# Graph attention over 16 batches: half-width masked tiles and a split store for the last batch, and a new hand-written front

## The chip, the cores and the metric

The kernel runs on one core of a Trainium2 chip. The metric is the device time of one execution in microseconds. TensorE (PE) does products and transposes into eight PSUM banks; VectorE (DVE), ScalarE (ACT) and GpSimd (POOL) do the element-wise work and reductions; SyncE (SP) and ScalarE issue DMAs. Each engine works through its own list in order and meets the others at semaphores.

## The reference

`x` is 16 batches of 512 nodes with 128 features, `adj` a 512 x 512 adjacency. Cut to what is computed:

```
def gat(inp, mask, W, a):
    h = inp @ W
    e = leaky_relu((h @ a_first)[:, :, None] + (h @ a_second)[:, None, :], 0.2)
    if mask is not None: e = where(mask > 0, e, -9e15)
    return elu(softmax(e, axis=2) @ h)

h   = relu(layernorm(x))
out = relu(h @ mlp1_w + mlp1_b)                       # 256 wide
out = elu(gat(out, None, W_fc, a_fc)) + out           # first attention, 256 wide
out = relu(out @ mlp2_w + mlp2_b)                     # 128 wide
out = relu(elu(gat(out, adj, W_hand, a_hand)) + out)  # second attention, masked
x   = x + out
x   = x + gat(relu(layernorm(x)), adj, W, a)          # third attention, masked
```

## The kernel before

Everything is fp32. A batch is four tiles of 128 nodes (`C` = 4). Each batch goes through the same steps, and a step is named `step.batch`: `stats1`, `root1`, `norm1` (or `normt`, on x loaded by features) for the first normalisation; `mlp1_0`, `mlp1_1` for the two 128-wide halves of the first dense layer, kept in `o1_t`; `h1_0` to `h1_3` for the products with `W_fc` of the four node tiles, evicted to `ext`; `max1`, `args1`, `row1` for the scores; `prob1_t` for the unnormalised attention of source tile t to all 512 targets; `att1_c` for the products of target tile c over the four source tiles; `elu1`, `z`, `mlp2`. The second attention is `h2`, `max2`, `args2`, `row2`, `prob2`, `att2`, `elu2`, `x1` (with `turn_o2`), then `norm2`, `root2`, `turn2`; the third is `h3`, `max3`, `args3`, `row3`, `prob3`, `att3`, `elu3`, and `result` writes `y_out`, which SyncE's step `result` stores.

A probability tile holds, for 128 sources in the partitions, all 512 targets in the columns. In the masked layers of batches 13 to 15 (`SCALED`, `HALVED`) ScalarE scales the row of the targets by the sources' factor (`scale_row`, L833), and VectorE takes the maximum with a second factor and the minimum with the mask (`prob_scaled`, L1177). For these batches the row stays in a PSUM bank, filled by four transposes (L1432). TensorE's `attend_masked` (L1493) makes two groups of products, q = 0 for target tiles 0 and 1, q = 1 for 2 and 3. It waits for each of the four probability tiles in turn at the first target tile, so its second target tile needs all four. The tails of the attention (`att3_q`, `elu3_q`, `result_q`) go in halves of 256 columns for batches 13 to 15.

What each engine does when is written out by hand: `ORDER` has one list per engine with every step of every batch, and `sequence` walks through it. A product takes the next of eight banks in the order of TensorE's list and waits until the reader of the step eight places earlier is done (`free`). `STIRRED` puts extra transposes of the identity in front of some steps (L1327), `WARM` seven at the start (L1322). Batch 0 is normalised by the steps `means` and `roots` (transposes of its moments, L1372), batches 1 and 2 by `norm1` and `turn1` (L1363), all others from moments that go through memory.

`edgeless` (L977 to L981) reduces the adjacency over its columns on VectorE; `empties` (L1352) turns its result, and `masks_0` to `masks_3` (L989) make the mask. `scores1` and `scores23` (L1335, L1343) fill the score columns of the weights.

A guard watches the range of the exponents. Its step `flag` (L1258, VectorE) writes `guard_flag`. At the end of its list every engine waits for it, loads it and branches past a general form of the network (L1542, L1543), then drains (L1558). SyncE first waits for all stores (L1541). The steps of VectorE's list end with `elu3_1.15 result_1.15 flag`.

## Time and profile before

| | us |
|---|---|
| median of 3 runs | 432.27 |
| lowest, highest | 432.2, 433.75 |
| profiled execution | 432.44 |
| its span | 430.6 |
| TensorE busy | 411.8 |
| VectorE busy | 358.1 |
| ScalarE busy | 314.4 |

The span runs from the first to the last instruction of the profiled execution; 1.8 us of its time lie outside. Busy time of TensorE is modelled with the end of each product, so products that follow each other overlap by some 0.16 us in the rows: how long a step holds the engine is read from the start of one to the start of the next. An fp32 product is two records, a transpose one.

### The profile page before, as it was taken

How to read it: one execution, taken by the hardware profiler on the slowest of the kernel's cores; microseconds unless marked ns; L12 is line 12 of the kernel's file. 1: busy time of each engine (PE TensorE's matmuls, PEld its weight loads, DVE VectorE, ACT ScalarE, POOL GpSimd, SP SyncE). 2: the span in 40 equal slices, each digit the busy share in tenths (PEclk: the TensorE clock that was granted, in tenths of full speed). 3: DMA queues.
4: the chain of work that ended last, by engine and by line, in shares of the span. 5: the costliest groups of instructions: out<-in, count | busy, mean ns of one | idle time of the engine just before them, and what ended most of it. 6: DMA issues, size and time to landing. Idle time of an engine off the chain costs nothing.

```text
span 430.6 us, 8695 instructions
## 1 busy us (share of the span) xinstructions
PE 411.8 (96%) x2545; PEld 353.0 (82%) x2545; DVE 358.1 (83%) x1222; ACT 314.4 (73%) x760; POOL 25.0 (6%) x53
## 2 busy tenths in 40 slices
PE   6899999999999999999999999999999999989782
PEld 4688788887888989797998788989889799869772
DVE  6788589968888898889898787987798989889973
ACT  2545867778876978686777878479678887799873
POOL 0000000000001000000100010100100110010000
PEclk9999999999999999999999999999999999999998
DMA  7745145142332123232321422223120223101101
GB/s 216 247 150 172 30 115 143 48 112 73 100 122 75 51 99 98 52 100 74 121 76 51 123 57 94 66 63 95 51 74 2 73 77 99 47 4 32 43 2 54
DMA packets 39445, 36.41 MB, mean 85 GB/s; under 512 B 4064, under 2 KB 30304, under 8 KB 39392
## 3 DMA queue, kind: packets, MB, share of 16 engines
q1 hardware_dynamic: 37392, 33.17, 25.8%
q10 hardware_dynamic: 2000, 2.63, 1.9%
q8 instruction: 22, 0.36, 0.3%
q14 instruction: 31, 0.25, 0.2%
HBM read 31.46 MB, written 4.32 MB: 83 GB/s over the span
## 4 chain that ended last, share of the span: by engine, by line
issue 66%; PE 20%; DVE 6%; POOL 5%; ACT 2%; POOLq 0%; DVEq 0%; ACTq 0%
PE bank L1403 6%; POOL fmax L713 5%; PE bank L1392 4%; PE bank L1493 3%; PE bank L1382 2%; DVE prob L1177 2%; PE bank L1421 1%; DVE u L1231 1%; PE bank L1443 1%; PE bank L1432 1%; DVE stats L1010 1%; PE bank L1411 1%; PE bank L1322 0%; ACT e L885 0%; PE bank L1372 0%
## 5 line engine op out<-in xcount | busy, mean ns | idle before, releaser
L1493 PEld LDWEIGHTS bank<-ext,prob 128*128 128x128 f32 x1024 | 119.6, 192 | 5.5 <-issue 3.1
L1493 PE MATMUL bank<-ext,prob 128*128 128x129 f32 x1024 | 122.6, 276 | 0.6 <-DVE prob L1177 0.3
L1403 PE MATMUL bank<-ext,prob 128*128 128x257 f32 x512 | 118.4, 380 | 0.0
L1403 PEld LDWEIGHTS bank<-ext,prob 128*128 128x128 f32 x512 | 95.0, 190 | 16.7 <-issue 4.2
L1177 DVE SCALAR_TENSOR_TENSOR prob<-prob,square,mask_t 128x512 f32<-128x512 f32 x102 | 73.5, 741 | 5.1 <-ACT prob L833 5.0
L1392 PE MATMUL bank<-wfc_sb,o_t 128*128 128x259 f32 x256 | 63.3, 382 | 0.0
L833 ACT ACTIVATE prob<-row,square 128x512 f32<-128x512 f32 x78 | 54.5, 721 | 0.7 <-DMA row<-row_scratch 0.6
L1392 PEld LDWEIGHTS bank<-wfc_sb,o_t 128*128 128x128 f32 x256 | 46.4, 191 | 9.2 <-issue 3.5
L1231 DVE SCALAR_TENSOR_TENSOR u<-e,y 128x512 f32<-128x512 f32 (+1 forms) x70 | 44.6, 639 | 9.5 <-issue 4.7
L877 ACT ACTIVATE y<-bank,recip 128x128 f32<-128x128 f32 x128 | 39.1, 366 | 16.5 <-DVE recip L1223 16.4
L885 ACT ACTIVATE e<-y,minus_one 128x512 f32<-128x512 f32 (+1 forms) x70 | 47.8, 686 | 1.1
L713 POOL PARTITION_ALL_REDUCE fmax<-fmax_col x48 | 24.3, 506 | 390.3 <-DVE fmax_col L1112 390.2
L866 ACT ACTIVATE y<-bank,recip 128x256 f32<-128x256 f32 x64 | 29.6, 465 | 11.7 <-DVE recip L1216 11.6
L889 ACT ACTIVATE e<-e,minus_one 128x512 f32<-128x512 f32 (+1 forms) x51 | 35.6, 697 | 2.4
L1382 PE MATMUL bank<-normed_t,w_sb 128*128 128x512 f32 x64 | 32.5, 594 | 0.0
L1158 DVE TENSOR_SCALAR prob<-row,square 128x512 f32<-128x512 f32 x64 | 32.3, 535 | 0.0
L1421 PE MATMUL bank<-z_t,w_sb 128*128 128x512 f32 x64 | 30.3, 596 | 0.3 <-DVE z_t L1238 0.3
L771 ACT ACTIVATE o_t<-bank,vec_sb 128x512 f32<-128x512 f32 x32 | 21.8, 688 | 10.9 <-issue 4.2
L779 ACT ACTIVATE ext<-bank 128x259 f32<-128x259 f32 x64 | 23.0, 384 | 6.3 <-issue 2.5
L817 ACT ACTIVATE square<-args 128x12 f32<-128x12 f32 x48 | 9.9, 207 | 22.8 <-DVE args L1133 12.1
L1238 DVE SCALAR_TENSOR_TENSOR z_t<-bank,o_t 128x512 f32<-128x512 f32 x32 | 21.5, 683 | 3.4 <-PE bank L1411 3.2
L807 ACT ACTIVATE ext<-bank,rstd 128x131 f32<-128x131 f32 x64 | 19.6, 370 | 3.7 <-PE bank L1443 2.4
(96 smaller groups left out, 496.6 us busy)
## 6 DMA issues: line engine op xcount, KB each, us to landing
row<-row_scratch SPq DMA_DIRECT2D x36, 256.0 KB, 3.3
moments_row<-moments_scratch SPq DMA_DIRECT2D x13, 512.0 KB, 3.9
x_in<-in_x SPq DMA_DIRECT2D x16, 256.0 KB, 4.7
x_res<-in_x SPq DMA_DIRECT2D x16, 256.0 KB, 4.2
out<-y_out SPq DMA_DIRECT2D x16, 256.0 KB, 3.7
normed<-in_x_t SPq DMA_DIRECT2D x14, 256.0 KB, 4.3
row_scratch<-square_t SPq DMA_DIRECT2D x144, 0.5 KB
adj_sb<-in_adj ACTq DMA_DIRECT2D x1, 1024.0 KB, 6.6
```

The lines of the kernel that those rows point to most:

```text
L713: nc.gpsimd.partition_all_reduce(L.fmax[:, b.slot], L.fmax_col[:, b.slot], P, bass.bass_isa.ReduceOp.max).then_inc(s.fmax.sem, 1)
L833: nc.scalar.activation(L.prob_of(b)[:, t], row_of(b, L), ACT.Copy, scale=L.buv[:, b.slot, 2, t:t + 1]).then_inc((s.scaled_first if t == 0 ...
L877: nc.scalar.activation(L.y[:, c], filled[:, e * (D + 3):e * (D + 3) + D], ACT.Copy, bias=1.0, scale=L.recip[:, b.slot, c:c + 1]).then_inc( ...
L885: nc.scalar.activation(L.e[:, r], L.y[:, r], ACT.Exp, bias=minus_one[:]).then_inc(s.exp.sem, 2 // parts)
L889: nc.scalar.activation(L.e[:, r], L.e[:, r], ACT.Exp, bias=minus_one[:]).then_inc(s.exp2.sem, 2 // parts)
L1177: nc.vector.scalar_tensor_tensor(out=p, in0=p, scalar=L.buv[:, b.slot, 1, t:t + 1], in1=mask_t[:, t], op0=ALU.max, op1=ALU.min).then_inc(s ...
L1231: nc.vector.scalar_tensor_tensor(out=L.u[:, r], in0=L.e[:, r], scalar=1.0, in1=L.y[:, r], op0=ALU.min, op1=ALU.max).then_inc(s.u.sem, 2 // ...
L1382: nc.tensor.matmul(filled[:], w1_sb[:, f * P:(f + 1) * P], normed_t[0][:, b.slot], start=True, stop=True).then_inc(o1_filled.sem, 1)
L1392: last = nc.tensor.matmul(filled[:, 0:H + 3], o1_t[:, b.of(O1_DEPTH), k, c * P:(c + 1) * P], wfc_sb[:, k], start=(k == 0), stop=(k == HT - 1))
L1403: last = nc.tensor.matmul(filled[:, 0:H + 1], gat1.targets(b, t, c), gat1.features_and_one(b, t), start=(t == 0), stop=(t == C - 1))
L1421: last = nc.tensor.matmul(filled[:], w2_sb[:, k], z_t[:, b.slot, k], start=(k == 0), stop=(k == HT - 1))
L1493: last = nc.tensor.matmul(filled[:, e * (D + 3):e * (D + 3) + D + 1], L.targets(b, t, c), L.features_and_one(b, t), start=(t == 0), stop=( ...
```

## The change

1. **Half tiles.** `CUT` names batch 15 for the third attention. There each of the four steps `prob3_t.15` makes two pieces of 256 columns: t = 0 the source tiles 0 and 1 for the first 256 targets, t = 1 the tiles 2 and 3 for the same targets, t = 2 and t = 3 the same for the other 256. That is 8 instructions of 256 columns on ScalarE and on VectorE each, where there were 4 of 512. `att3_0.15` waits for the first two steps only, `att3_1.15` for the last two.
2. **Store in halves.** The store of batch 15 is two DMAs, the first as soon as `result_0.15` is done, with a semaphore of its own.
3. **Front by hand.** On TensorE `h1_0.0` and `h1_1.0` stand ahead of `turn1.1`, `h1_2.0` and `h1_3.0` behind it and ahead of `mlp1_0.1`. Stirring before `roots.0` is two transposes, not three. `scores23` is 11 places later, `empties` behind `att1_0.0`. ScalarE evicts `mlp1_0.0` and `mlp1_1.0` before `root1.1`.
4. **Order elsewhere.** The five lists hold the same steps as before, but are listed anew. On TensorE a step moves by 1.4 places in the mean, on ScalarE and VectorE by 2.4. In VectorE's list `flag` stands ahead of `result_0.15`.

```diff
+CUT = {1: (), 2: (15,)}
-STIRRED = {("roots", 0): 3, ("mlp1_0", 0): 3, ("row3", 14): 10, ("turn2_half", 15): 6, ("h3_0", 15): 4}
+STIRRED = {("roots", 0): 2, ("mlp1_0", 0): 3, ("row3", 14): 10, ("turn2_half", 15): 6, ("h3_0", 15): 4}
...
     "scalar": """
-        weights root1.0 root1.1 mlp1_0.0 mlp1_1.0 turn1.1 root1.2 adjacency mlp1_0.1 h1_0.0 mlp1_1.1 h1_1.0
+        weights root1.0 mlp1_0.0 mlp1_1.0 root1.1 h1_0.0 h1_1.0 turn1.1 adjacency root1.2 mlp1_0.1 mlp1_1.1
...
     "tensor": """
-        warm means.0 roots.0 scores1 mlp1_0.0 mlp1_1.0 turn1.1 h1_0.0 mlp1_0.1 h1_1.0 mlp1_1.1 h1_2.0 h1_3.0
+        warm means.0 roots.0 scores1 mlp1_0.0 mlp1_1.0 h1_0.0 h1_1.0 turn1.1 h1_2.0 h1_3.0 mlp1_0.1 mlp1_1.1
...
+        s_half_stored = semaphore("last_batch_half_stored")
...
+        def cut(b, L):
+            return L.masked and not b.passed and b.n in CUT[L.k]
+
+        def cut_parts(t):
+
+            return (2 * (t % 2), 2 * (t % 2) + 1), slice(t // 2 * (N // 2), (t // 2 + 1) * (N // 2))
...
             def store(b):
+                rest = slice(0, C)
+                if not general and b.n == B - 1:
+                    sp.wait_ge(*y_ready.at(b, 1))
+                    sp.dma_start(out_v[b.n][:, 0:C // 2], y_out[:, b.slot, 0:C // 2]).then_inc(s_half_stored, 16)
+                    rest = slice(C // 2, C)
                 sp.wait_ge(*y_ready.at(b, 2))
-                sp.dma_start(out_v[b.n], y_out[:, b.slot]).then_inc(stored.sem(b), 16)
+                sp.dma_start(out_v[b.n][:, rest], y_out[:, b.slot, rest]).then_inc(stored.sem(b), 16)
...
+                if cut(b, L):
+                    tiles, half = cut_parts(t)
+                    for k in tiles:
+                        last = nc.scalar.activation(L.prob_of(b)[:, k, half], row_of(b, L)[:, half], ACT.Copy,
+                                                    scale=L.buv[:, b.slot, 2, k:k + 1])
+                    last.then_inc((s.scaled_first if t == 0 else s.scaled_row).sem, 1)
+                    return
...
+                if cut(b, L):
+                    tiles, half = cut_parts(t)
+                    for k in tiles:
+                        p = L.prob_of(b)[:, k, half]
+                        last = nc.vector.scalar_tensor_tensor(out=p, in0=p, scalar=L.buv[:, b.slot, 1, k:k + 1],
+                                                              in1=mask_t[:, k, half], op0=ALU.max, op1=ALU.min)
+                    last.then_inc(s.prob_ready.sem, 1)
+                    return
...
-                        if c == 0 and factored(L, general):
+                        if not general and cut(b, L):
+                            if e == 0 and t % 2 == 0:
+                                pe.wait_ge(*s.prob_ready.at(b, 2 * q + t // 2 + 1))
+                        elif c == 0 and factored(L, general):
                             pe.wait_ge(*s.prob_ready.at(b, t + 1))
...
+                sp.wait_ge(s_half_stored, 16)
```

Where the order changes, the instructions now stand as follows (line numbers of the changed kernel are 33 or so higher). TensorE's queue from the first-layer products of batch 0 (`w_sb`, L1382 and L1415) to its fourth `ext` product (`wfc_sb`, L1392 and L1425), before:

```order
L1382 MATMUL bank<-normed_t,w_sb 128x512 x2
L1363 MATMUL bank<-ident,normed 128x128 x4
L1392 MATMUL bank<-wfc_sb,o_t 128x259 x2
L1382 MATMUL bank<-normed_t,w_sb 128x512
L1392 MATMUL bank<-wfc_sb,o_t 128x259 x2
L1382 MATMUL bank<-normed_t,w_sb 128x512
L1392 MATMUL bank<-wfc_sb,o_t 128x259 x6
L1363 MATMUL bank<-ident,normed 128x128 x4
```

and in the changed kernel:

```order
L1415 MATMUL bank<-normed_t,w_sb 128x512 x2
L1425 MATMUL bank<-wfc_sb,o_t 128x259 x4
L1396 MATMUL bank<-ident,normed 128x128 x4
L1425 MATMUL bank<-wfc_sb,o_t 128x259 x4
L1415 MATMUL bank<-normed_t,w_sb 128x512 x2
L1396 MATMUL bank<-ident,normed 128x128 x4
L1425 MATMUL bank<-wfc_sb,o_t 128x259 x2
```

All four steps `h1_c.0` (two products each) now stand ahead of `mlp1_0.1`, and only one set of transposes lies between `mlp1_1.1` and `h1_0.1`.

ScalarE's queue at the same place: the two evictions of batch 0 (`o_t`), the square root of batch 1 (`log_var`, `guess`) and the eviction of its transposes (`normed_t`), before:

```order
L746 ACTIVATE log_var<-moments_n,ln_eps 128x4
L749 ACTIVATE guess<-log_var,ln_guess 128x4
L771 ACTIVATE o_t<-bank,vec_sb 128x512 x2
L756 ACTIVATE normed_t<-bank 128x512
L746 ACTIVATE log_var<-moments_n,ln_eps 128x4
```

and in the changed kernel:

```order
L789 ACTIVATE o_t<-bank,vec_sb 128x512 x2
L764 ACTIVATE log_var<-moments_n,ln_eps 128x4
L767 ACTIVATE guess<-log_var,ln_guess 128x4
L797 ACTIVATE ext<-bank 128x259 x2
L774 ACTIVATE normed_t<-bank 128x512
```

The root of batch 1 has moved from ahead of the two evictions to behind them.

VectorE's queue at its end, from the probability tiles of batch 15 on, before:

```order
L1177 SCALAR_TENSOR_TENSOR prob<-prob,square,mask_t 128x512 x4
L1254 TENSOR_REDUCE guard_col<-guard 128x1
L1223 RECIPROCAL recip<-bank 128x2
...
L1231 SCALAR_TENSOR_TENSOR u<-e,y 128x256
L1247 SCALAR_TENSOR_TENSOR y_out<-u,x 128x256
L1258 TENSOR_SCALAR guard_flag<-guard_all 128x1
L1542 TENSOR_LOAD guard_flag
```

and in the changed kernel:

```order
L1206 SCALAR_TENSOR_TENSOR prob<-prob,square,mask_t 128x256 x4
L1256 RECIPROCAL recip<-bank 128x2
L1206 SCALAR_TENSOR_TENSOR prob<-prob,square,mask_t 128x256 x4
L1287 TENSOR_REDUCE guard_col<-guard 128x1
...
L1291 TENSOR_SCALAR guard_flag<-guard_all 128x1
L1280 SCALAR_TENSOR_TENSOR y_out<-u,x 128x256
L1264 SCALAR_TENSOR_TENSOR u<-e,y 128x256
L1280 SCALAR_TENSOR_TENSOR y_out<-u,x 128x256
L1578 TENSOR_LOAD guard_flag
```

The four tiles have become eight halves with a reciprocal of batch 14 between them, and the flag is written three instructions before the last `y_out`.

## Rows read from the trace of the kernel before

**Rows 1.** The page, part 1: busy us, share of the span, instructions.

```profile
PE 411.8 (96%) x2545; PEld 353.0 (82%) x2545; DVE 358.1 (83%) x1222; ACT 314.4 (73%) x760; POOL 25.0 (6%) x53
```

**Rows 2.** Busy us of PE, PEld, DVE, ACT, POOL (instructions), clock, DMA share, GB/s, by stretch.

```profile
200.00:250.00 50.00, 50.00 (x314) 43.33 (x313) 43.34 (x133) 40.02 (x94) 2.98 (x5) 1.00 0.30 91
...
380.00:400.00 20.00, 18.02 (x148) 16.63 (x148) 17.87 (x46) 18.88 (x46) 1.90 (x3) 1.00 0.10 28
...
420.00:431.00 11.00, 3.17 (x26) 2.98 (x26) 3.52 (x14) 3.42 (x10) 0.52 (x1) 0.82 0.18 54
```

**Rows 3.** Waits of PE from 40 to 400 us: us in total, times, longest.

```profile
PE bank L1411 <- DVE u L1231: 1.7, 1, 1.7
```

**Rows 4.** Timeline of PE in front: start us, us, what, records, idle before it.

```profile
6.18 0.85 PE L1327 MATMUL bank<-ident 128*128 128x128 f32 x3
...
8.63 1.88 PE L1382 MATMUL bank<-normed_t,w_sb 128*128 128x512 f32 x4
12.07 0.66 PE L1363 MATMUL bank<-ident,normed 128*128 128x128 f32 x4 [1.56 <-DVE normed L1052]
12.56 1.04 PE L1392 MATMUL bank<-wfc_sb,o_t 128*128 128x259 f32 x4
13.44 1.10 PE L1382 MATMUL bank<-normed_t,w_sb 128*128 128x512 f32 x2
...
15.25 1.02 PE L1382 MATMUL bank<-normed_t,w_sb 128*128 128x512 f32 x2
...
25.66 3.63 PE L1403 MATMUL bank<-ext,prob 128*128 128x257 f32 x16
```

**Rows 5.** Timeline of ACT and DVE in front.

```profile
9.65 0.30 ACT L746 ACTIVATE log_var<-moments_n,ln_eps 128x4 f32<-128x4 f32 x1 [3.71 <-DVE moments_n L1015]
10.18 1.25 ACT L771 ACTIVATE o_t<-bank,vec_sb 128x512 f32<-128x512 f32 x2
10.90 1.11 DVE L1052 TENSOR_SCALAR normed<-x_in,moments_n,rstd 128x128 f32<-128x128 f32 x4
...
16.31 0.69 ACT L771 ACTIVATE o_t<-bank,vec_sb 128x512 f32<-128x512 f32 x1 [0.77 <-PE bank L1382]
...
21.35 2.28 DVE L977 TENSOR_REDUCE has_edge<-adj_sb 128x4 f32<-128x2048 int32 x1
...
26.15 0.54 DVE L1158 TENSOR_SCALAR prob<-row,square 128x512 f32<-128x512 f32 x1
```

**Rows 6.** Timeline of PE from 380 to 387 us: the two starts behind a wait.

```profile
381.88 1.09 PE L1411 MATMUL bank<-ident,u 128*128 128x128 f32 x8 [1.67 <-DVE u L1231]
...
384.62 1.98 PE L1421 MATMUL bank<-z_t,w_sb 128*128 128x512 f32 x4 [0.31 <-DVE z_t L1238]
```

**Rows 7.** Timeline of the tail; the L866 row: duration ns min/median/max, first and last start.

```profile
416.55 2.42 ACT L833 ACTIVATE prob<-bank,square 128x512 f32<-128x512 f32 x4 [0.80 <-PE bank L1432]
417.27 2.74 DVE L1177 SCALAR_TENSOR_TENSOR prob<-prob,square,mask_t 128x512 f32<-128x512 f32 x4 [1.30 <-ACT prob L833]
...
420.06 3.17 PE L1493 MATMUL bank<-ext,prob 128*128 128x129 f32 x26 [0.17 <-DVE prob L1177]
...
425.13 0.42 DVE L1247 SCALAR_TENSOR_TENSOR y_out<-u,x 128x256 f32<-128x256 f32 x1
425.48 0.15 DVE L1258 TENSOR_SCALAR guard_flag<-guard_all 128x1 int32<-128x1 f32 x1
...
L866 ACT ACTIVATE y<-bank,recip x64: 452/466/491, 30.3 to 379.1; 128x256 f32<-128x256 f32 x64
```

**Rows 8.** The engines' way out (L1543, L1558): duration ns, start us.

```profile
L1543 PEldq COMPARE_BRANCH  x1: 3672/3672/3672, 426.6 to 426.6; - x1
...
L1558 SPq DRAIN  x1: 45/45/45, 429.2 to 429.2; - x1
...
L1558 DVEq DRAIN  x1: 63/63/63, 429.7 to 429.7; - x1
L1558 PEldq DRAIN  x1: 73/73/73, 430.4 to 430.4; - x1
```

More of the change, by code:

```diff
@@ L109 @@
[L109 to L111 removed]
+        weights root1.0 mlp1_0.0 mlp1_1.0 root1.1 h1_0.0 h1_1.0 turn1.1 adjacency root1.2 mlp1_0.1 mlp1_1.1
+        turn1.2 root1.3 h1_2.0 h1_3.0 h1_0.1 args1.0 h1_1.1 root1.4 h1_2.1 row1.0 h1_3.1 mlp1_0.2 mlp1_1.2
@@ L211 @@
-        turn_o2.15 h3_0.14 h3_1.14 row3.14 turn2.15 h3_0.15 h3_1.15 att3_0.14 row3.15 att3_1.14 att3_0.15
-        att3_1.15
+        warm means.0 roots.0 scores1 mlp1_0.0 mlp1_1.0 h1_0.0 h1_1.0 turn1.1 h1_2.0 h1_3.0 mlp1_0.1 mlp1_1.1
+        turn1.2 h1_0.1 mlp1_0.2 h1_1.1 h1_2.1 row1.0 h1_3.1 mlp1_1.2 att1_0.0 empties row1.1 h1_0.2 h1_1.2
+        att1_1.0 att1_2.0 att1_3.0 h1_2.2 att1_0.1 h1_3.2 scores23 z_0.0 att1_1.1 mlp1_0.3 z_1.0 att1_2.1
+        mlp1_1.3 mlp2.0 att1_3.1 h2_0.0 h1_0.3 h1_1.3 row1.2 h2_1.0 h1_2.3 h1_3.3 z_0.1 mlp1_0.4 z_1.1 att1_0.2
```

306 lines of the change are left out of this document (153 added, 153 removed).

## Prediction

> **What bounds the kernel now.** I read the share of each engine first [rows 1], then the busy time by stretch [rows 2], then what TensorE waited for between 40 and 400 us [rows 3], and last the instructions in order of time at the three places that the change names [rows 4 to 8]. TensorE is busy 96% of the span. In a stretch of the middle it is busy 50.00 of 50 us at the full granted clock, and over 360 us its one wait of size is 1.7 us, in front of the two transposes `z_0.15`, `z_1.15` [rows 2, 3]. So between 12 and 380 us the kernel is a full TensorE queue. A new order of the same products can win almost nothing there; it can only open holes. Time is to be had in front, where TensorE idles 1.56 us before `turn1.1` [rows 4], at the 1.67 us wait [rows 6], and in the tail, where products, VectorE (17.87 of 20 us) and ScalarE (18.88 of 20) hand one batch to and fro [rows 2]. After the last `y_out` there are 5.1 us more in which no tile is computed [rows 7, 8].
>
> **Front, TensorE.** Four pieces follow from the new order. (a) One stirring transpose less ahead of `roots.0`: three take 0.64 us (6.18 to 6.82 by their starts), so `mlp1_0.0` starts 0.21 earlier, at 8.42 instead of 8.63, provided its input is ready. It is, since `normt.0` now stands ahead of the memsets of `ones`. (b) `h1_0.0` needs both `o1_t` tiles evicted. From the start of such a product to the end of its eviction it is 15.25 to 16.31 + 0.69 = 17.00, so 1.75 us [rows 4, 5], and a product occupies TensorE for 0.86. `mlp1_1.0` starts at 9.28, so `h1_0.0` starts at 11.08 after 0.94 idle. `h1_0.0` and `h1_1.0` take 0.88 each (12.56 to 13.44), to 12.84. (c) `root1.1` now stands behind the two evictions on ScalarE, not ahead of them. It started at 9.65; the evictions last 1.25 and now end about 11.03, so it starts at 10.93, 1.28 later, and the last `normed` tile of batch 1 ends at 12.01 + 1.28 = 13.29 [rows 5]. `turn1.1` starts at 13.34, after 0.50 idle, and takes 0.49 (12.07 to 12.56). (d) `h1_2.0`, `h1_3.0`, `mlp1_0.1` fill to 16.45, when `mlp1_1.1` starts. Behind it stands only `turn1.2` before `h1_0.1` needs the eviction: 16.45 + 1.75 = 18.20, while TensorE is free at 17.8. That is 0.45 idle where there was none, because `h1_2.0` and `h1_3.0` used to stand there. `h1_0.1` ends at 19.13. Before, the same set of products was done at 19.17 (17.86 + 0.88 + 0.43 for `turn1.2`). Three small holes have replaced one: a gain of 0.04, not of 1.56.
>
> **Front, VectorE.** `att1_0.0` moves ahead of `scores23`, `empties` and `h1_0.2` (0.36 + 0.47 + 0.88 = 1.71), so TensorE is at it at 25.66 - 1.71 - 0.04 = 23.91 [rows 4]. Its fourth product starts 1.30 later, at 25.21, and needs `prob1_3.0`. That ended at 26.69 [rows 5], on a VectorE queue that the reduction of the adjacency (2.28 us) holds up in both orders. `masks_0` and `scores23` no longer stand ahead of it (0.60 + 0.14 by their steps), and `args1.0` comes about 0.3 earlier, since ScalarE has `h1_3.0` done sooner: 25.65 to 25.95. A hole of 0.45 to 0.75; I take 0.5. **The front therefore costs 0.46 us**, with bounds of -1.5 (all idle gone) and +1.2.
>
> **The middle.** Every batch's steps are re-listed, mostly by one to three places. Lengths don't change, and the holes there sum to 2.0 us (1.67 and 0.31) [rows 3, 6]. No row prices a hole that isn't there yet; the nearest are these two, and the lower bound is no hole. I take 0.1, nearer to nothing, since where I compared the products between a step and the step that needs its result, almost every distance stays above the delay that the trace shows. At 380 us ScalarE now runs `root2.13` ahead of `att1_2.15` and `att1_3.15`. It costs 0.6, of which a wait takes 0.2 to 0.3; so `z_0.15` and `mlp2.15` come 0.3 later than 381.88 and 384.62 [rows 6]. VectorE has waits of some 0.3 at `max3.13` and at `args3.13` behind that, which absorb most: 0.1. **Together +0.2**, bounds 0 and +5.
>
> **The tail.** `row3.15` is there at 416.55 in both. Halves of 256 columns: ScalarE takes 0.466 for 256 and 0.69 for 512 [rows 7], and successive ones overlap by 0.11 (2.42 for four), so halves start every 0.36. Eight end at 416.55 + 7 x 0.36 + 0.47 = 419.54, against 418.97 for four whole ones. VectorE takes 0.42 for 256 columns. The first 256 targets are ready after two pairs, at 418.10 + 0.03 + 0.34 + 0.42 = 418.89; the last pair at 420.33, against 420.01. TensorE: 13 products (26 records) took 3.17 from 420.06 on, 0.223 each. Six products of `att3_0.15` follow 418.94, to 420.28, and eight of `att3_1.15` run on behind them, to 422.22 with the last one's drain, against 423.23. So TensorE gains 1.0, though both vector engines lose 0.3 to 0.6. ScalarE is next: from 419.54 it has four pairs of `y` (0.63 each, less 0.1 for the first) and four `e` of 0.51, which makes 4.4, so its last `e` ends at 423.95. Then `u` and `y_out` on VectorE, 0.03 + 0.42 + 0.03 + 0.42: the last `y_out` ends at **424.85 instead of 425.55**, 0.70 earlier.
>
> The Trainium skill ("VectorE: DVE Perf Modes", section "The TRN2 errata — SBUF-src ops pay a fixed extra latency per instruction") speaks against the split: a fixed cost per instruction, so cut no finer than 512 elements. The rows agree (0.466 for half of what takes 0.69). Taken alone it would put the end of the last masked tile 0.3 later and forecast a loss; what outweighs it is that the second `prob` half no longer stands ahead of the first products.
>
> **The exit.** After its last step each engine loads the guard flag and branches past the general network. TensorE's branch lasts 3.67 us and its drain comes at 430.4, just ahead of the end; VectorE's drain comes at 429.7, SyncE's, which waits for the store, at 429.2 [rows 8]. TensorE starts this at `guard_flag`, 425.48, which is 5.17 before the end. In the new order `flag` stands ahead of `result_0.15`, so it comes about 423.2, and TensorE would be done at 428.4. VectorE must first do its last `y_out`: from its last instruction (425.63) to its drain it took 4.15, and from the last drain to the end 0.26. So 424.85 + 4.4 = 429.25. SyncE: the drain is 3.7 behind `y_out`, with 0.3 to the end: 428.85, less what half a store saves (bounds 0 and 1.9; it hides behind VectorE). **The span ends at 429.25 instead of 430.65: -1.4.**
>
> This trace has a branch of 3.67 us on TensorE, and 2.8 to 3.1 us between branch and drain on ScalarE and VectorE. The Trainium skill ("Advanced Engine Details and Errata", "Control Flow Timing") has about 108 ns for a compare-and-branch; by that SyncE's chain alone would set the end and the gain would be the 0.7 of `y_out`. The row decides against it.
>
> **Sum.** 432.44 + 0.46 + 0.2 - 1.4 = 431.7. The profiled execution lay 0.17 above the median of 432.27, so 431.5 to 431.7 as a median; I say 431.7, -0.1%. A measurement of this kernel can tell about 0.5%, 2.16 us, from no change.
>
> **Rivals.** (1) *The front pays as its idle time suggests.* If `prob1_3.0` and the evictions come in time, the 1.56 us hole goes and nothing takes its place: 431.7 - 0.5 - 1.4 = 429.8. For it: the hole is real. Against it: the 1.75 us from product to eviction. Chance 0.15. (2) *The new listing opens waits in the middle (slower).* Its place is a product such as `z_0.15`, whose input comes over ScalarE and VectorE queues that are over 80% full; its price is 1.67 us each time [rows 6]. The forecast turns into a loss from the first such hole on; two of them make 435.0. Against it: the waits of 2.0 us in 360 show what such listings reach. Chance 0.15. (3) *The exit isn't moved.* If VectorE's way out lasts as long as TensorE's when it starts last (5.2 instead of 4.4), the gain is that of `y_out`, 0.7: 432.4. Chance 0.2. (4) *The clock falls.* The granted clock is 1.00 (2.4 GHz) through the front and falls only after the last product [rows 2]. The longest idle time in front shrinks from 1.56 to 0.94, so I give it 0.03; 2.2 us of products at 1.2 GHz cost 2.2: 433.9. The forecast itself has 0.42, between 430.9 and 432.3; 0.05 is left for a middle that wins some.
>
> **Chances and range.** Faster by over 0.5% (under 430.1): rival 1 and part of the rest, 0.19. Slower (over 434.4): most of rival 2 and little of 4, 0.14. Within: 0.67. The range is 429.9 to 434.2; it leaves out most of rival 2 and the edge of rival 1.
>
> **What would show it.** Front: idle time of TensorE ahead of `h1_0.0` (0.9), `turn1.1` (0.5), `h1_0.1` (0.45) and inside `att1_0.0` (0.5). Middle: the list of TensorE's waits between 40 and 400 us; over 3 us in it is rival 2. Tail: last product 1.0 closer to the start of the eight halves, last `y_out` 0.7. Exit: the last drain is VectorE's, 4.15 behind its last `y_out`. Wrong at once if the last drain is still TensorE's, or if TensorE starts `att1_0.0` without a hole.

## The result: 434.78 us, slower than forecast, and the profile after

| | before | changed |
|---|---|---|
| median | 432.58 (20 runs) | 434.78 (20 runs) |
| lowest, highest | 432.09, 434.21 | 432.43, 436.87 |
| ratio | | 1.0031, 95% interval 1.0017 to 1.0046 |
| profiled execution, its span | 432.44, 430.6 | 433.27, 431.5 |

The changed kernel is 0.3% slower by the ratio and 2.2 us by the medians; that is still within the 0.5% that I called no change, but 434.78 is outside the range of 429.9 to 434.2. The ratio and the medians differ because the times of both kernels fall in **two groups**, and the median jumps when the larger group changes. Over all measurements made for this study the kernel before has 96 runs from 431.9 to 432.9 and 52 from 433.3 to 435.0, and none between. The changed kernel has 10 of 26 from 432.4 to 433.5 and 16 from 434.6 to 436.9. Its profiled execution belongs to the lower group, so the profile below shows only part of the loss.

The waits of TensorE in the changed kernel: from the list over the whole span the four that lie in the new front, then the whole list between 40 and 400 us (us in total, times, longest):

```profile
PE bank L1436 <- DVE prob L1183: 1.2, 1, 1.2
PE bank L1425 <- ACT o_t L789: 0.9, 1, 0.9
PE bank L1360 <- DMA w_sb<-in_L_gnn_mlp_w: 0.3, 1, 0.3
PE bank L1396 <- DVE normed L1077: 0.2, 1, 0.2
...
PE bank L1444 <- DVE u L1264: 1.7, 1, 1.7
```

The last row is the only one between 40 and 400 us, as in [rows 3]: the re-listing opened nothing in the middle. The other four are the new front. Its timeline on TensorE, then VectorE (start us, us, what, records, idle before it):

```profile
8.70 0.55 PE L1360 MATMUL bank<-ident 128*128 128x128 f32 x3 [0.35 <-DMA w_sb<-in_L_gnn_mlp_w]
9.08 1.88 PE L1415 MATMUL bank<-normed_t,w_sb 128*128 128x512 f32 x4
11.84 1.99 PE L1425 MATMUL bank<-wfc_sb,o_t 128*128 128x259 f32 x8 [0.87 <-ACT o_t L789]
14.00 0.66 PE L1396 MATMUL bank<-ident,normed 128*128 128x128 f32 x4 [0.17 <-DVE normed L1077]
...
26.01 2.04 PE L1436 MATMUL bank<-ext,prob 128*128 128x257 f32 x8 [1.18 <-DVE prob L1183]
...
22.73 2.29 DVE L1002 TENSOR_REDUCE has_edge<-adj_sb 128x4 f32<-128x2048 int32 x1 [0.93 <-DMA adj_sb<-in_adj]
```

The `w_sb` products start at 9.08, not at 8.63 as in [rows 4]: their weights landed 6.4 us after the issue, 5.4 before. The hole ahead of `att1_0.0` is 1.18 us (1.34 by the starts of the steps), because the adjacency was issued 1.1 us later (14.70 against 13.59) and landed 8.0 us after that (6.6 before). To compare the two orders behind that, take the points at which TensorE has done the same set of products in both, the stirring left out. There the changed kernel is 2.34 us behind from 40 to 75 us, 2.0 from 115 to 145, 1.83 from 330 to 375, and 1.54 at 416. So the front costs 2.3 us, and the re-listed steps behind it give 0.8 back, most of it in pieces under 0.2 us that the list of waits doesn't show.

The tail, and the issue of the last store:

```profile
418.09 3.03 ACT L854 ACTIVATE prob<-bank,square 128x256 f32<-128x256 f32 x8 [0.80 <-PE bank L1465]
418.97 1.67 DVE L1206 SCALAR_TENSOR_TENSOR prob<-prob,square,mask_t 128x256 f32<-128x256 f32 x4 [1.46 <-ACT prob L854]
...
425.98 0.43 DVE L1280 SCALAR_TENSOR_TENSOR y_out<-u,x 128x256 f32<-128x256 f32 x1
426.44 0.37 SPq L705 DMA_DIRECT2D out<-y_out  x1
```

From the start of ScalarE's masked tiles to the end of the last `y_out` it is 8.32 us (426.41 - 418.09), against 9.00 before (416.55 to 425.55, [rows 7]): the 0.7 that was forecast. The way out: TensorE's branch, SyncE's wait for the last half store, the drains (duration ns, start us):

```profile
L1579 PEldq COMPARE_BRANCH  x1: 3702/3702/3702, 426.4 to 426.4; - x1
...
L1577 SPq EVENT_SEMAPHORE  x1: 2330/2330/2330, 427.5 to 427.5; - x1
...
L1594 DVEq DRAIN  x1: 63/63/63, 429.9 to 429.9; - x1
L1594 PEldq DRAIN  x1: 73/73/73, 430.2 to 430.2; - x1
L1594 SPq DRAIN  x1: 45/45/45, 431.2 to 431.2; - x1
```

In [rows 8] SyncE's drain was first and TensorE's last. Now SyncE's is last. From the last `y_out` to the end it is 5.07 us (426.41 to 431.48), as before (5.09).

### The profile page after: what moved, and what is told of

Same layout as the page of the kernel before. It is cut to its first block, busy times and chain, and to the rows that moved or that the text cites. A ratio compares the mean times of both kernels' runs of the same rounds, so it can differ in the third digit from the quotient of the medians.

```text
span 431.5 us, 8704 instructions
## 1 busy us (share of the span) xinstructions
PE 411.9 (95%) x2544; PEld 352.3 (82%) x2544; DVE 357.8 (83%) x1226; ACT 316.0 (73%) x764; POOL 24.9 (6%) x53
## 4 chain that ended last, share of the span: by engine, by line
PE 84%; DMA 5%; DVE 4%; ACT 3%; issue 2%; SPq 1%; POOL 0%; ACTq 0%; DVEq 0%
PE bank L1529 24%; PE bank L1436 23%; PE bank L1425 11%; PE bank L1476 6%; PE bank L1454 6%; PE bank L1415 6%; PE bank L1444 3%; DMA adj_sb<-in_adj 2%; PE bank L1537 2%; DMA w_sb<-in_L_gnn_mlp_w 1%; PE bank L1495 1%; PE bank L1465 1%; DMA row<-row_scratch 1%; DVE u L1264 1%; ACT ext L825 1%
## 5 line engine op out<-in xcount | busy, mean ns | idle before, releaser
L1210 DVE SCALAR_TENSOR_TENSOR prob<-prob,square,mask_t 128x512 f32<-128x512 f32 x98 | 70.7, 739 | 1.0 <-ACT prob L858 0.8
L1425 PE MATMUL bank<-wfc_sb,o_t 128*128 128x259 f32 x256 | 64.1, 382 | 0.9 <-ACT o_t L789 0.9
L1425 PEld LDWEIGHTS bank<-wfc_sb,o_t 128*128 128x128 f32 x256 | 46.2, 190 | 10.4 <-issue 5.0
L797 ACT ACTIVATE ext<-bank 128x259 f32<-128x259 f32 x64 | 23.9, 382 | 12.5 <-PE bank L1425 10.6
L1415 PE MATMUL bank<-normed_t,w_sb 128*128 128x512 f32 x64 | 32.0, 592 | 0.0
```

Of the source, the lines that this page charges most:

```text
L1210: nc.vector.scalar_tensor_tensor(out=p, in0=p, scalar=L.buv[:, b.slot, 1, t:t + 1], in1=mask_t[:, t], op0=ALU.max, op1=ALU.min).then_inc(s ...
L1415: nc.tensor.matmul(filled[:], w1_sb[:, f * P:(f + 1) * P], normed_t[0][:, b.slot], start=True, stop=True).then_inc(o1_filled.sem, 1)
L1425: last = nc.tensor.matmul(filled[:, 0:H + 3], o1_t[:, b.of(O1_DEPTH), k, c * P:(c + 1) * P], wfc_sb[:, k], start=(k == 0), stop=(k == HT - 1))
```

## Experiments

All times are medians of device time. The kernel before ran beside each set (432.5 beside e1 to e4, 433.3 beside e5 to e8, 432.4 beside e9 to e12, 432.5 beside e13 and e14, 432.8 beside e15). Its median moves with the share of its upper group, so the tables also say how many runs lie in which group.

### Undoing parts: e1 to e4

e1, the flag last again (VectorE's list):

```diff
-        ... result_1.14 elu3_0.15 flag result_0.15 elu3_1.15 result_1.15
+        ... result_1.14 elu3_0.15 result_0.15 elu3_1.15 result_1.15 flag
```

> The changed kernel with one step moved: the guard flag is written after the last y_out again, not three instructions before it. Theory A (the early flag sends TensorE, ScalarE and GpSimd off to fetch code while the last half store is under way; 24 or so of its packets come up to 2 us late on one DMA engine): the store lands 2.3 us after its issue again instead of 3.4, and TensorE's branch of 3.7 us is the end again, 5.0 to 5.2 us after the flag. With y_out ending at 426.4 the span ends at 431.5 or a little under, within 0.3 us of the changed kernel: what the store gains, the branch takes. Rival B (the store is slow because it is a half, not because of the fetches): it lands 3.4 us after its issue here too, and the span is as long as with the early flag or up to 0.1 longer.

e2, the adjacency issued earlier (ScalarE's list):

```diff
-        ... mlp1_1.0 root1.1 h1_0.0 h1_1.0 turn1.1 adjacency root1.2
+        ... mlp1_1.0 root1.1 adjacency h1_0.0 h1_1.0 turn1.1 root1.2
```

> The changed kernel with ScalarE's two adjacency loads issued ahead of the eviction of h1_0.0, not behind turn1.1. Theory A (the front lost 1.35 us because the adjacency was issued at 14.70 instead of 13.59 and landed only 8.0 us later, so that the reduction over it and all four first probability tiles came late): the issue comes at about 12.3, the reduction starts when args1.0 is done (21.8) instead of 22.7, TensorE's wait before att1_0.0 shrinks from 1.34 to 0.4 or less, and the median falls by 0.9 us. Rival B (the front is bound by something else, such as the x loads that now share the DMA engines with it): the wait stays above 1 us and the median moves by less than 0.3.

e3, the changed kernel with the steps that the kernel before starts in its first 45 us in their old order, and the changed lists behind them:

```diff
-STIRRED = {("roots", 0): 2, ...
+STIRRED = {("roots", 0): 3, ...
     "tensor": """
-        warm means.0 roots.0 scores1 mlp1_0.0 mlp1_1.0 h1_0.0 h1_1.0 turn1.1 h1_2.0 h1_3.0 mlp1_0.1 mlp1_1.1
+        warm means.0 roots.0 scores1 mlp1_0.0 mlp1_1.0 turn1.1 h1_0.0 mlp1_0.1 h1_1.0 mlp1_1.1 h1_2.0 h1_3.0
```

> The changed kernel with the old lists up to 45 us (and three stirring transposes before roots.0), the new lists behind that. Theory A (the front costs 1.5 to 1.8 us, the middle nothing): the median is 1.5 us below that of the changed kernel, and the tail reads as in it, 0.85 - 1.8 = about 1 us ahead of the kernel before at the last product. Rival C (the re-listed middle or the tail costs it): the median stays within 0.5 us of the changed kernel.

e4, the kernel before with the half tiles of batch 15 alone: old lists, whole store, flag last.

```diff
-                if not general and b.n == B - 1:
+                if False:
...
-                sp.wait_ge(s_half_stored, 16)
```

> The kernel before with one thing changed: the last masked tiles of batch 15 in halves of 256 targets, all lists as before, the store whole, the flag last. Theory A (halves bring the last y_out 0.7 us forward, as they did between the same points of the changed kernel, and the exit follows the flag at 5.17 us): 0.7 us faster than before, 431.8 against 432.5. Rival D (in the old list the reciprocal of att3_1.14 stands behind all halves, and ScalarE and VectorE lose to the cut what TensorE gains): within 0.3 us of before.

| | median | ratio to before, interval | span of the profiled one |
|---|---|---|---|
| e1 flag last | 432.68 | 1.0013 (0.9997 to 1.0029) | 432.4 |
| e2 adjacency early | 435.76 | 1.0078 (1.0055 to 1.0101) | 433.8 |
| e3 old front | 433.02 | 1.0008 (0.9995 to 1.0021) | 431.5 |
| e4 half tiles alone | 433.16 | 1.0001 (0.9990 to 1.0013) | 431.8 |

**e2** shows that the later issue of the adjacency was no mistake to be mended by an earlier one. The adjacency landed 6.0 us after its issue at 11.66, so by 17.7. But its two matrices (2 MB) then stood ahead of the loads of x, and the load that follows in VectorE's list came 3 us late. VectorE's rows of e2:

```profile
21.56 0.87 DVE L1037 BATCH_NORM_STATS2 stats<-x_in 128x6 f32<-128x128 f32 x4 [3.09 <-DMA x_in<-in_x]
...
23.86 2.28 DVE L1004 TENSOR_REDUCE has_edge<-adj_sb 128x4 f32<-128x2048 int32 x1
```

The reduction starts at 23.86, later than in the changed kernel (22.73). From 14 to 21 us e2 moves 358 to 377 GB/s without a pause, as the kernel before does (343 to 406) from 17 to 23; whoever goes first there, the other waits. The order of the loads is not all that e2's median holds. Behind an idle stretch of 1.95 us TensorE's granted clock fell to 0.50, its lower level, from 25.0 to 28.4 us (start us, us, what, records, idle before it; then a stretch: us, busy and records, clock, DMA share, GB/s):

```profile
24.34 0.62 PE L1467 MATMUL bank<-ident,square 128*128 128x128 f32 x4 [1.95 <-ACT square L837]
...
25.00:26.00 1.00, 1.00 (x4) 0.50 0.02 2
```

In these 3.4 us its products took twice as long, up to 1.7 us lost by that (an estimate from the two numbers). Of e2's six runs the two slowest (437.3 and 437.6) have a mean granted clock of 0.986, the two fastest (434.4 and 435.0) 0.997 and 0.996. **e3** didn't isolate the front: where the two orders were joined, at 47 to 50 us, TensorE waited 1.3 us that neither kernel has, about as much as the old front saved. I draw nothing from its median. Its trace does show the lists behind the front alone: by the work done it is 1.62 us behind the kernel before from 50 to 75 us and 0.88 at 409, so they give 0.7 back here too.

**e1** and **e4** had a surprise in the trace. In both, the first `w_sb` products take twice as long as in the profiles of before and after, and all that follows is later for it: e4 has the front of the kernel before, step by step, and starts `h1_0.0` at 13.93 instead of 12.56. This became the main question, below.

For **the way out** e1 gives a clear answer. With the flag last, TensorE's branch is last to end, and the same half store lands 1.8 us after its issue instead of 3.4. The DMA view of the changed kernel from 426.4 to 429.9 us, then of e1 over the same piece, from the store's issue to its landing (427.5 to 429.45):

```profile
q1 hardware_dynamic: 618, 0.29, 28.5%
q8 instruction: 1, 0.02, 2.2%
q14 instruction: 3, 0.02, 2.2%
...
out<-y_out SPq DMA_DIRECT2D x1, 128.0 KB, 3.4
```

```profile
q1 hardware_dynamic: 627, 0.30, 50.2%
q14 instruction: 1, 0.01, 1.6%
...
out<-y_out SPq DMA_DIRECT2D x1, 128.0 KB, 1.8
```

`q8` and `q14` carry code (instruction packets), `q1` the store. In the changed kernel a 16 KB code packet runs beside the store, with the last packets of the store behind it; in e1 no `q8` packet does. So the early flag sends TensorE out earlier and lets its code fetch fall on the store. The other profiles bear it out: with the flag last the last half store lands after 1.8 us (e1, e10, e15), and in all nine kernels with store halves and an early flag after 2.8 to 4.1.

### The way out and the front: e5 to e7

e5, the flag one step earlier still, where VectorE idles:

```diff
-        ... elu3_1.14 att3_1.15 result_1.14 elu3_0.15 flag result_0.15
+        ... elu3_1.14 flag att3_1.15 result_1.14 elu3_0.15 result_0.15
```

> The changed kernel with VectorE's flag one step earlier still: ahead of the reciprocal of the last product (about 423.9 in the profile after, where VectorE idles) instead of at 425.07. Theory A: the changed kernel's last half store landed 3.4 us after its issue (before: 2.3) because TensorE's branch, 0.8 us after it began, fetched code over the same DMA engines just as the store's packets started (the 16 KB packet of the fetch at 427.25, the store's from 427.3). With the flag 1.2 us earlier the fetch is over when the store starts; the store lands in 1.9 to 2.3 us, VectorE's drain is last, the exit is y_out's end plus 3.7 to 4.0 us instead of 5.04, and the median 1.0 to 1.3 us under the changed kernel's: 433.5 to 433.8, or 431.4 to 431.7 where the front had a good execution. Rival B: an early fetch always meets one half or the other, the last half store still takes 3.4 us and the exit stays at 5.0: 434.8. Rival C: the store isn't slowed by the fetch but by being a half: then e1's 1.84 us for the same half could not be.

e6, all lists of the kernel before, with half tiles, half stores and e5's place of the flag:

```diff
 ORDER = the lists of the kernel before, but in "vector":
-        ... elu3_1.14 result_0.14 att3_1.15 result_1.14 elu3_0.15 result_0.15 elu3_1.15 result_1.15 flag
+        ... elu3_1.14 result_0.14 flag att3_1.15 result_1.14 elu3_0.15 result_0.15 elu3_1.15 result_1.15
```

> The kernel before's step lists in full (front, middle, tail), with the changed kernel's half tiles and half stores of batch 15, and the flag ahead of the reciprocal of the last product. Against e5_flag_first it differs by the front and the re-listed middle alone. Theory A: the hand-made front costs what the two traces showed at 380 us, 1.8 us: this kernel is 1.5 to 2.0 us under e5, 430.6 to 431.6 us in the median, and beats both kernels (before: 432.5). Rival B: those 1.8 us were the luck of one profiled execution (how fast loads landed), and the re-listing is worth nothing either way: equal to e5 within 0.4 us. Against the kernel before: the halves save 0.4 to 0.7 us at y_out, the exit up to 1.3 more.

e7, the 256 KB of `load_again.0` behind `load.8` again on SyncE:

```diff
-        ... weights_rest load_again.0 load.4 load_t.3 ... load.8 load_again.1 load_t.5
+        ... weights_rest load.4 load_t.3 ... load.8 load_again.1 load_again.0 load_t.5
```

> The changed kernel with SyncE's load_again.0 (256 KB) back where it stood before, behind load.8, and nothing else. Theory A: those 256 KB ahead of the adjacency made its landing take 8.0 us instead of 6.6, and so TensorE's hole ahead of att1_0.0 1.34 us instead of the 0.5 forecast: the hole shrinks to about 0.5, and the median falls by 0.6 to 0.8 us, to about 434.0. Rival B: the adjacency's landing varies by itself (6.6, 7.0 and 8.0 us in three traces with the old list of loads), and it is its later issue, 14.70 instead of 13.59, that counts: no change beyond 0.3 us, 434.5 to 435.0.

| | median | runs in the lower, upper group | from last `y_out` to the end, profiled |
|---|---|---|---|
| e5 flag first | 433.88 | 5, 7 | 4.6 |
| e6 old lists, new end | 432.60 | 3, 9 | 4.5 |
| e7 load back | 433.12 | 8, 4 | 5.4 |

**e5**: neither theory in full. TensorE was done 2.5 us before the end, but the code fetch now met the *first* half of the store, which took 3.3 us, and the last half 3.0. The exit gained 0.4, not 1.3. **e7** answers its question: the adjacency again took 8.0 us to land, and the hole ahead of `att1_0.0` stayed:

```profile
PE bank L1438 <- DVE prob L1185: 1.2, 1, 1.2
```

The 256 KB ahead of it weren't the cause (rival B). The same old list of loads gave 6.6, 7.0, 8.0 and 6.2 us (before, e4, e3, e6). What the new front changed is the issue (14.51 here, 14.70 in the changed kernel, 13.59 before), because `adjacency` stands behind the eviction of `turn1.1` on ScalarE and that waits for TensorE. The issue isn't the whole of it: in e10 (below) the adjacency was issued at 13.68, nearly as early as before, landed 8.0 us later, and the hole was 1.1 us all the same.

### When the products become fast: e8 and e14

In the profile of the kernel before the first products (128 columns) take 213 ns from start to start where they follow each other, from 3.61 to about 7.2 us; from then on 109. The 512-column products of `w_sb` take 429. In e1, e4 and e6 the change came only at 12.5 to 12.9 us, and the same products took 853. The two lengths stand nearly as 2 to 1, like the two levels of TensorE's clock, 1.2 and 2.4 GHz. The granted-clock column doesn't show the first rise: ahead of it the column says 1.00 in every profile, so there only the length of products tells. Later falls it does show: products of 853 ns stand beside 0.50 in e15, below. e8 brings work of TensorE forward, e14 takes some away, both on the kernel before:

```diff
+        cold = sb("cold", [P, P])          # e8; set to zero by GpSimd as its first instruction
...
             def warm(b):
+                pe.wait_ge(s_cold, 1)
+                for _ in range(6):
+                    nc.tensor.matmul(bank[7][:, 0:P], cold[:], cold[:], start=True, stop=True)
```

```diff
-WARM = 7                                   # e14
+WARM = 0
```

> The kernel before with TensorE busy from about 1.0 us instead of 3.6: six products of a zeroed tile ahead of the seven on the identity. Nothing else. The times of every kernel here fall in two groups (before: 432.0 to 432.9 and 433.3 to 434.3). In the traces the products of the front take twice as long until about 7.1 us (before, after), 7.9 (e2), 8.1 (e3) or 12.4 (e1, e4), and where that is 12.4 all that follows is 1.4 us later with the old front, 2.0 with the new. Theory A: the two groups are these two moments, and they depend on when TensorE's work begins: with 2.6 us more of it ahead they come earlier, under 8.6 us in nearly every execution, the upper group goes, and the median falls by 0.1 to 0.5 us, to 432.0 to 432.4. Rival B: the groups have another cause, or the moment doesn't follow the start of the work: a third of the runs stays 1.4 us above the others, the median 432.5.

> The kernel before without its seven warm products (TensorE begins at about 5.2 us instead of 3.6), the other side of e8: e8 put work ahead and the upper group went. Theory A: the moment from which products run at double rate follows the start of TensorE's work; begun 1.6 us later it falls at 8.7 us or later, in more executions only at 12.4, and the upper group grows: half or more of the runs above 433.3, the median 433.3 to 434.0. Rival B: only the idle stretch ahead of 1.0 us counts, or the moment is fixed in time: the same shares as the kernel before beside it, within chance (a third above 433.3), the median 432.3 to 432.7.

| | TensorE begins at | fast products from (profile) | runs in the lower, upper group | median |
|---|---|---|---|---|
| e8 | 1.0 us | 4.8 us | 12, 0 | 432.21 |
| before, all measurements | 3.6 | 7.2 | 96, 52 | |
| e14 | 5.1 | 14.8 | 0, 8 (from 433.26) | 434.00 |

TensorE's timeline of e8, at the start and at the products of `mlp1_0.0` and `mlp1_1.0`, then the same products in e14:

```profile
0.99 2.93 PE L1323 MATMUL bank<-cold 128*128 128x128 f32 x12 [0.99 <-POOL cold L1572]
3.71 1.49 PE L1326 MATMUL bank<-ident 128*128 128x128 f32 x7
5.07 0.65 PE L1376 MATMUL bank<-ident,moments_n 128*128 128x128 f32 x4
...
8.60 1.88 PE L1386 MATMUL bank<-normed_t,w_sb 128*128 128x512 f32 x4
```

```profile
9.76 3.62 PE L1382 MATMUL bank<-normed_t,w_sb 128*128 128x512 f32 x4
```

Four records of `w_sb`, 1.88 or 3.62 us; and four of 128 columns at 5.07 in 0.65, where e14's at 5.14 take 1.08. Theory A held on both sides: every kept profile with slow `w_sb` products (e1, e4, e6, e13, e14, and e15 below) belongs to the slower runs of its kernel, so the upper group **is** the late moment, and how early TensorE has work moves how often it comes. No upper run of the kernel before itself was profiled; e4 and e6 have its front. e8 costs nothing and is faster than the kernel before (0.9982, 0.9967 to 0.9997).

### The parts again, with the moment early: e9 to e12, e15

These carry e8's six products, which take nearly all runs out of the upper group. e9 is the changed kernel with them, e10 is e1 with them, e11 is e6 with them, e12 is e4 with them, and e15 is e11 with the flag last.

> The changed kernel, all of it, with the six early products of e8 ahead of TensorE's first ones, and nothing else. In e8 they brought the moment at which products run at double rate from 7.1 or later to 4.8 us, all 12 runs of the kernel before then lay between 431.96 and 432.93, and the upper group was gone. Theory A: the changed kernel's median of 434.78 is two things, a real cost of about 0.8 us (front +1.8, tail -0.7, exit 0, start -0.3), which its lower group shows (432.4 to 433.5, median 433.1), and an upper group 2.1 us higher with half of its runs in it, which comes from the late moment alone. Then this kernel has one group, median 432.7 to 433.2, nothing above 434. Rival B: the upper group of the changed kernel has another cause too, the landing of loads in the new front or of the last store: runs from 434.5 to 436 stay, the median is 433.5 to 434.8.

> e9 with the flag at the end of VectorE's list, as in e1. Differs from e9 by the place of the flag alone, with the clock's part taken out. Theory A: the early flag gains nothing: what TensorE's branch gains (0.4 to 1.2 us) is lost to the store, which lands 3.4 us after its issue instead of 1.8: this kernel is equal to e9 within 0.3 us (profiles: exits 5.04 with the flag early and 4.83 with it last). Rival B: the early flag costs 0.5 us or more, since in the changed kernel's lower group the median was 433.1 and in e1's 432.4: this kernel 0.5 to 0.8 under e9.

> e6 (the lists of the kernel before, the halves of batch 15, half stores, flag ahead of the last reciprocal) with the early products. Against e9 and e10 it differs by the hand-made front and the re-listed middle (and the flag's place). Theory A: the front costs 1.4 to 1.8 us: this kernel 431.0 to 431.6, in one group (e6's three lowest runs were 431.24 to 431.42), 1.3 or more under e9 and about 0.8 to 1.2 us under the kernel before in the median. Rival B: the front costs less than 0.5 us once the late moment is out: 431.8 to 432.5.

> e4 (the kernel before with batch 15's masked tiles by halves, whole store, flag last) with the early products. Against e11 it differs by half stores and the early flag, against e8 by the halves of the masked tiles. Theory A: the halves are worth the 0.70 us that y_out gained in the trace, less what TensorE's branch varies: 0.4 to 0.7 under e8's 432.2, 431.5 to 431.8; and e11 is a further 0.1 to 0.5 lower (exits of 4.5 and 4.6 in e5 and e6 against 5.04 and 5.35). Rival B: half stores and early flag are worth nothing: equal to e11 within 0.15 us.

> e11 with the flag at the end of VectorE's list. It is also e10 with the lists of the kernel before instead of the changed ones, and e12 with the store in halves. Theory A: the lists are what costs: 0.5 to 0.7 us under e10's 432.17, 431.5 to 431.7; half stores with the flag last are worth nothing (equal to e12's 431.58 within 0.15), since TensorE's way out is last there, and the flag ahead of the last reciprocal is worth 0.2 to 0.4 with these lists (e11: 431.28). Rival B: the difference between e10 and e12 was the half store and not the lists: this kernel at 432.0 to 432.3.

| | lists | half tiles | store | flag | median | lowest to highest | ratio to before, interval |
|---|---|---|---|---|---|---|---|
| e8 | old | no | whole | last | 432.21 | 431.96 to 432.93 | 0.9982 (0.9967 to 0.9997) |
| e12 | old | yes | whole | last | 431.58 | 431.47 to 432.81 | 0.9980 (0.9968 to 0.9992) |
| e15 | old | yes | halves | last | 431.70 | 431.32 to 432.84 | 0.9970 (0.9959 to 0.9980) |
| e11 | old | yes | halves | first | **431.28** | 431.10 to 431.63 | 0.9972 (0.9961 to 0.9984) |
| e10 | new | yes | halves | last | 432.17 | 431.48 to 432.78 | 0.9988 (0.9976 to 0.9999) |
| e9 | new | yes | halves | as changed | 432.42 | 431.85 to 432.86 | 0.9998 (0.9988 to 1.0007) |

Only e9 to e12 ran in one set. The lower group of the kernel before was at 432.31 beside them and beside e8, but at 432.58 beside e15 (10 runs), so e15 is read by its distance from that group: 0.88 under it, where e8 is 0.10, e12 0.73, e11 1.03 and e10 0.14 under theirs and e9 0.11 above. So the half tiles save 0.63 us (e8 to e12). The store in halves and the flag ahead of the last reciprocal save 0.30 together (e12 to e11, one set); e15 would give 0.15 to each, too little to tell them apart. The flag where the change put it costs 0.25 (e10 to e9). The new lists cost 0.74 (e15 to e10; 0.47 by the bare medians). The traces agree: by the work done TensorE is 0.69 us behind at 416 us in e10 against e11, and 0.62 in e9 against e12. The whole change costs 0.21 (e8 to e9). Differences of 0.1 to 0.3 us are near what these medians can tell; those of 0.6 and more are beyond it.

The lists' price is less than the 1.1 to 1.8 us that the traces had led me to expect. In e9 and e10 the front costs 1.4 us by the work done, where it cost 2.3 in the first profile, and the lists behind it give 0.7 to 0.8 of that back. e9's expectation was half right: no run above 432.9, so no other cause of an upper group shows, but the median was 0.3 to 0.8 under what I expected, since the early moment also shortened the new front (`att1_0.0` at 24.77 instead of 26.01).

**The six products make slow `w_sb` products rare, they don't rule them out.** The profiled execution of e15 is its slowest, 432.84, 1.1 us above its median. Its TensorE ran fast from 5.5 us, stood idle three times for 0.2 to 0.4 us, and fell back to the lower level from 8.9 to 12.3 us, the granted clock at 0.50, just for the `w_sb` products:

```profile
8.85 0.90 PE L1366 MATMUL bank<-ident 128*128 128x128 f32 x3 [0.44 <-DMA w_sb<-in_L_gnn_mlp_w]
9.54 3.26 PE L1421 MATMUL bank<-normed_t,w_sb 128*128 128x512 f32 x4
...
9.00:10.00 1.00, 1.00 (x4) 0.50 0.81 231
```

e12's highest run, 432.81, stands 0.9 above the next and may be another; it wasn't profiled. So what sets the upper group is the rate of the products in the front, be it by a late rise or, as here, by a fall. None of the other 67 runs with these products stands so far apart.

**e11 beats both kernels**: 431.28, 1.0 us under the lower group of the kernel before. Its last drains:

```profile
L1600 PEldq DRAIN  x1: 73/73/73, 427.7 to 427.7; - x1
L1600 DVEq DRAIN  x1: 61/61/61, 428.3 to 428.3; - x1
L1600 SPq DRAIN  x1: 45/45/45, 429.0 to 429.0; - x1
```

### The changed kernel once more: e13

> The changed kernel as it is, a second time, for what the early products of e9 leave open: 11 of its 20 runs lay above 434.6, 9 under 433.5, while of 118 runs of the kernel before 43 lay above 433.3 and 75 under 432.9. Theory A: how often the late moment comes is a matter of the execution, not of the change; a late one costs the old front 1.45 us and the new one 2.1, since its first three h1 wait for the double length of mlp1_0.0 and mlp1_1.0 with nothing between. Then the share above 434.3 is again that of the kernel before beside it, a third to a half, the lower group stands at 432.4 to 433.5, the upper at 434.6 to 436, and where the profiled execution is a late one its products run slow until about 12.4 us. Rival B: the changed kernel falls into the late moment more often by its own doing: a share above 434.3 of two thirds or more, with the kernel before at a third.

Median 434.78 over 6 runs, again, and 1.0044 (1.0027 to 1.0061) of the kernel before; five of six in the upper group, where the kernel before had 2 of 13. The profiled execution is from the upper group, 1.8 us above the first one. Its products, then its busy time and clock from 9 to 12 us (us, busy and records, clock, DMA share, GB/s):

```profile
9.72 3.11 PE L1415 MATMUL bank<-normed_t,w_sb 128*128 128x512 f32 x4
13.70 1.99 PE L1425 MATMUL bank<-wfc_sb,o_t 128*128 128x259 f32 x8 [0.87 <-ACT o_t L789]
```

```profile
9.00:12.00 3.00, 3.00 (x7) 1.00 0.79 218
```

Fast products come at 12.2 us. `h1_0.0` starts at 13.70 instead of 11.84, and of these 1.87 us 1.5 are left where the last masked tiles start. In the old front a late moment moves `h1_0.0` by 1.37 (e4) to 1.51 (e6), and no further wait takes any of it back. The rest of the upper group's height, 2.05 us between the changed kernel's two medians (433.09 and 435.14) against 1.43 for the old front (432.35 and 433.78), I can't place in a row: in e13 0.3 of it is the exit (5.4 us instead of 5.1).

**What stays open**: whether the new front makes the late moment more frequent. 16 of 26 runs against 52 of 148 looks like it, but other kernels with the same front had 3 (e1), 7 (e5) and 4 (e7) of 12, and with the old front e4 had 7 and e6 9 of 12. The kernel before itself had from 2 of 13 (beside e13) to 18 of 35 (beside e5 to e8), so the share also differs from set to set. Up to 6.2 us the instructions of TensorE stand within 0.2 us of each other in all of them.

## Why the prediction was wrong, point by point

- **What bounds the kernel**: right. From 45 to 380 us TensorE has no wait in the list in either profile, and its one wait of size, 1.7 us, is the same.
- **Front, start**: failed. I had `mlp1_0.0` 0.21 us earlier, "provided its input is ready", and looked only at `normt.0` for that. The other input is the weights, which landed at 8.65 us: 0.45 later than before instead of 0.21 earlier. In e5, where they came in time (7.47 us), the term holds: 8.44, with 8.42 forecast.
- **Front, the small holes**: right in place and size. Forecast 0.94, 0.50 and 0.45 us ahead of `h1_0.0`, `turn1.1` and `h1_0.1`; by the starts of the steps they are 1.03, 0.33 and 0.47, the last in two parts around `turn1.2`.
- **Front, `att1_0.0`**: the step that failed by most. I took 0.5, bounds 0.45 to 0.75, from VectorE's queue alone, and held the reduction of the adjacency where it was ("holds up in both orders"). It waits for a DMA that ScalarE issues behind `turn1.1`, which the new order delays. The hole was 1.2 us (1.34 by the starts), 1.2 in e7, 1.1 in e10, 0.4 in e9 and 0.3 in e1. With 0.66 from the start it is most of what took the front from the 0.46 forecast to 2.3 us in the profile, also beyond my bound of +1.2; in e9 and e10 the front cost 1.4.
- **The middle**: no hole opened, as forecast, but the sign of the term was wrong. I put it at +0.2 with a lower bound of nothing, since the waits that the list shows sum to 2.0 us. The new lists gave 0.8 back: 0.5 by 375 us and 0.3 more by 416. They gave 0.7 to 0.8 in e9, e10 and e3 too. Part of it can be seen in the starts: from 46 to 375 us the kernel before has 13 places where the next product starts over 40 ns later than it mostly does behind such a one (0.98 us in all), the changed kernel 7 (0.56 us).
- **Tail**: the sum was right to 0.02 us (0.68 of 0.70 gained at `y_out`). The parts were a little off: VectorE's halves last 0.48, not 0.42, and TensorE gained 0.7, not 1.0; ScalarE was indeed what set the end. e12 confirms it in the median: 0.63.
- **The way out**: failed. I forecast TensorE's drain out of the way, VectorE's last, 4.4 us behind `y_out`, and let SyncE hide behind it at 3.7 "less what half a store saves (bounds 0 and 1.9)". Both ends of that bound were gains. The half store took 1.1 us more than the whole one did, since the earlier flag brought TensorE's code fetch onto it, and SyncE's drain came last. Rival 3 named the outcome, the gain of `y_out` alone, but by another mechanism, VectorE's. VectorE in fact drained 3.5 us behind `y_out`, 0.7 sooner than I had it, since its flag no longer stood between; that would have paid, had SyncE come in time.
- **The clock**: rival 4 asked whether the clock would fall, and read 1.00 off the granted-clock column. But that column says 1.00 ahead of the first rise whatever the products do, and in a third of the executions the clock *rises* late, at 12 us or later; no term of the sum had that. That it can fall too is shown by e15 and e2, not by the changed kernel. [rows 4] showed it: 0.21 us per transpose at 6.18 (three in 0.64), where those from 12.07 take 0.11. So the profiled execution of before was one of the lower group and "0.17 above the median", and I set its front beside a changed front that pays more when the moment is late.

In numbers, for the profiled execution against the forecast of 431.7: the front 2.34 instead of 0.46 is +1.88, the lists behind it -0.80 instead of +0.2 are -1.00, `y_out` +0.02, the way out 5.07 instead of 4.40 is +0.67; together +1.57, which is the 433.27 that was measured. What the middle gave thus hid half of what the front missed, and that was luck. From there to the median of 434.78 it is the late moment, in 11 of 20 runs.

## What to carry to other kernels

Before two orders of a front are compared by one profile each, measure the length of one product shape through the first 15 us: if it halves somewhere, the moment varies from execution to execution, and a few products on a zeroed tile while the engine idles anyway cost nothing here and made the late runs rare (one or two of 69, against 52 of 148). When two orders of the same queue are compared, compare them where the same work is done: the list of waits missed 0.8 us that this shows. When a step is moved on a queue, follow the DMA issues behind it to whoever reads them. And where engines leave a kernel through a branch, their code fetches use the same DMA engines as the last store: an earlier exit of one engine can delay the one that waits for the store.

## What the runs showed of the hardware that I had not expected

- Products at half rate until 4.8 to 7 us with TensorE busy from 1.0 (e8 to e12, e15), until 7.2 to 12.9 from 3.6, until 14.8 from 5.1 (e14), with a granted clock of 1.00 in every row ahead of that rise. After it the column follows: 0.50 from 8.9 to 12.3 us in e15, behind idle pieces of 0.2 to 0.4 us, and from 25.0 to 28.4 in e2, behind 1.95 us. The Trainium skill ("TensorE: Matmul & The Clock Gate", part 1 on the clock gate) says that the moment differs from run to run of one kernel, and this case agrees. It also calls the cost under 1% of a kernel and nothing to fit; here it is 1.4 to 2 us, 0.3 to 0.5%, so under 1%, yet more than all that the change was about.
- A 128 KB store landed 1.8 us after its issue alone (the last one of e1, e10 and e15) and 2.8 to 4.1 beside a code fetch (the last one of nine kernels with an early flag).
- TensorE's branch out of the kernel took 3.5 to 4.4 us over the 17 profiles, the largest single piece of the way out.
- The 1 MB of the adjacency took 6.0 to 8.0 us to land, and as much with one and the same list of loads (6.0 in e15, 8.0 in e3).
